# Second attention: value rows broadcast from a copy in DRAM, and the residual x added by TensorE

## The reference

```python
qkv = x @ W_qkv.T                       # 16 heads of 8 features
q = (elu(q) + 1) * scale;  k = elu(k) + 1
for each chunk of 32 tokens:            # causal, state S (8 x 8 a head), Z (8)
    attn = (q @ k.T) * causal
    num = attn @ v + q @ S
    den = attn.sum(-1) + q @ Z
    S = S + k.T @ v;  Z = Z + k.sum(0)
out = num / maximum(den, 1e-6)
x = x + out @ W_out.T
```

## Time and profile before

| | |
|---|---|
| median of 3 runs | 689.75 us (688.23 to 690.7) |
| profiled execution | 690.44 us, its span 688.7 us |
| busy: PE / DVE / ACT / POOL | 378.3 / 424.8 / 219.6 / 358.2 us |
| second attention, first to last period's start | 366.70 to 479.89 us |

### The profile page before, as it was taken

How to read it: one execution, slowest core, us unless ns; L and a number is a source line. 1 busy time by engine, 2 the same in 40 slices (tenths; PEclk the granted TensorE clock), 3 DMA queues, 4 the chain that set the end, 5 groups by cost and what they waited for, 6 DMA issues and landing times.

```text
span 688.7 us, 7801 instructions
## 1 busy us (share of the span) xinstructions
PE 378.3 (55%) x2174; PEld 267.1 (39%) x2174; DVE 424.8 (62%) x1214; ACT 219.6 (32%) x531; POOL 358.2 (52%) x390
## 2 busy tenths in 40 slices
PE   4896755074331678676035667776743217866740
PEld 4554322071111567566012344443321116756640
DVE  6788999997888022123265789999787871222120
ACT  2577000036741122213015334433157312222110
POOL 6037960004100768888214888888740006888753
PEclk9999978577555689988556677877875557999885
DMA  5880000005061223334909988888460712333322
GB/s 148 321 306 0 0 1 0 0 12 172 2 138 2 54 38 45 43 41 36 251 3 121 128 133 131 133 133 131 71 184 0 138 2 53 37 46 45 43 22 19
DMA packets 63721, 54.80 MB, mean 80 GB/s; under 512 B 14656, under 2 KB 52160, under 8 KB 62400
## 3 DMA queue, kind: packets, MB, share of 16 engines
q1 hardware_dynamic: 45824, 44.20, 30.9%
q0 software_dynamic: 11264, 8.99, 10.0%
q10 hardware_dynamic: 6592, 1.15, 1.0%
HBM read 22.27 MB, written 15.27 MB: 55 GB/s over the span
## 4 chain that ended last, share of the span: by engine, by line
DVE 27%; POOL 18%; DMA 17%; issue 15%; PE 13%; ACT 3%; another core or an unknown queue 3%; SPq 2%; DVEq 1%; ACTq 0%; POOLq 0%
DVE arena L1234 11%; DMA arena<-arena 10%; POOL out L531 6%; POOL acc L531 6%; POOL arena L518 3%; DVE arena L1239 3%; DVE tk L1239 3%; DMA out<-arena,idx 2%; PE ps L941 2%; DVE bst L1246 2%; DMA acc<-arena,idx 2%; POOL tb L594 2%; PE ps L1044 1%; DMA tab<-tb 1%
## 5 line engine op out<-in xcount | busy, mean ns | idle before, releaser
L1234 DVE TENSOR_TENSOR arena<-ps,arena 128x256 f32<-128x256 f32 (+1 forms) x82 | 34.1, 425 | 148.0 <-DMA out<-arena,idx 68.3
L518 POOL DMA_INDIRECT arena<-tab,idx x64 | 62.8, 982 | 79.5 <-DMA tab<-tb 30.6
L757 ACT ACTIVATE arena<-ps,b 128x256 f32<-128x256 f32 x128 | 50.1, 474 | 149.5 <-PE ps L1106 135.7
L1106 PE MATMUL ps<-arena,f1w 128*128 128x256 f32 x256 | 74.0, 441 | 14.4 <-DVE arena L1238 12.5
L594 POOL TENSOR_TENSOR tb<-arena 128x512 f32<-128x512 f32 x64 | 70.8, 1122 | 10.1 <-PE ps L1167 9.2
L1116 PE MATMUL ps<-f2w,arena 128*128 128x128 f32 x512 | 65.7, 282 | 6.2 <-issue 4.3
L1116 PEld LDWEIGHTS ps<-f2w,arena 128*128 128x128 f32 x512 | 65.2, 199 | 9.5 <-issue 7.3
L531 POOL DMA_INDIRECT out<-arena,idx x32 | 51.0, 1594 | 24.3 <-DMA out<-arena,idx 12.4
L1106 PEld LDWEIGHTS ps<-arena,f1w 128*128 128x128 f32 x256 | 54.1, 222 | 24.3 <-DVE arena L1238 14.1
L1234 DVE TENSOR_TENSOR arena<-arena 128x256 f32<-128x256 f32 (+22 forms) x109 | 56.8, 555 | 2.2
L531 POOL DMA_INDIRECT acc<-arena,idx x32 | 50.5, 1579 | 13.5 <-issue 8.2
(11 more groups left out here) (265 smaller groups left out, 924.1 us busy)
## 6 DMA issues: line engine op xcount, KB each, us to landing
arena<-arena SPq DMA_DIRECT2D x64, 256.0 KB, 7.2
tab<-tb SPq DMA_DIRECT2D x8, 576.0 KB, 9.0
f1w<-in_f1T SPq DMA_DIRECT2D x4, 1024.0 KB, 12.2
f2w<-in_f2T SPq DMA_DIRECT2D x4, 1024.0 KB, 14.2
acc<-tb SPq DMA_DIRECT2D x8, 256.0 KB, 19.0
arena<-in_f2b SPq DMA_DIRECT2D x2, 1024.0 KB, 5.8
acc<-xs SPq DMA_DIRECT2D x8, 256.0 KB, 6.1
xs<-acc SPq DMA_DIRECT2D x8, 256.0 KB, 6.4
```

Source lines behind the costliest of these rows:

```text
L518: pool.indirect_dma_start(out=XE[:, e % RX, h, :], out_offset=None, in_=tab[f], in_offset=bass.IndirectOffsetOnAxis(ap=idx[:, i:i + 1], ax ...
L757: last = nc.scalar.activation(hT[:, e % 2, t, :], ps[:, 2 * (e % 2) + t // 2, (t % 2) * CAP:(t % 2 + 1) * CAP], ACT.Gelu, bias=b1[:, e, t: ...
L1106: last = nc.tensor.matmul(ps[:, 2 * (e % 2) + t // 2, (t % 2) * CAP:(t % 2 + 1) * CAP], f1w[:, e, t * P:(t + 1) * P], xeT[:, e % 2, :], st ...
L1234: return nc.vector.tensor_tensor(o, a, b, op)
```

## The change

Two edits, independent of each other. First, the values of a group are stored to a DRAM tensor `vd` by one DMA (128 x 512, 256 KB), SP waits until it has landed, and then the eight broadcast DMAs read their rows from `vd`. Only product 0 of group 0 still reads `vT`, and is issued ahead of the first store. Second, `add_out` of DVE is gone. `project_out` on PE now first multiplies the identity with x (128 x 512) into the PSUM bank, and the output projection accumulates on it. ACT copies the sum back to `xs` (`keep_x`), and DVE only takes the statistics (`take_stats`).

```diff
+    vd = nc.dram_tensor("vd", [NG, P, GW], F32).ap()
...
+            def replicate(n, values, i):
+                e = 2 * (i % 4) + i // 4
+                rows = values[e * NH:(e + 1) * NH, :]
+                sp.dma_start(VR[:, i, :], rows.rearrange("h (a t) -> h a t", a=1).to_broadcast([NH, HD, GW])).then_inc(vr_in[i], 16)
             for n in range(NG):
                 sp.wait_ge(v_kept, n + 1)
-                for i in range(HD):
+                if n == 0:
+                    replicate(0, vT[:, 0, :], 0)
+                sp.dma_start(vd[n], vT[:, n % 2, :]).then_inc(v_stored, 16)
+                sp.wait_ge(v_stored, 16 * (n + 1))
+                for i in range(1 if n == 0 else 0, HD):
                     if n >= 1:
                         sp.wait_ge(state_ready, (n - 1) * HD + i + 1)
-                    e = 2 * (i % 4) + i // 4
-                    rows = vT[e * NH:(e + 1) * NH, n % 2, :]
-                    sp.dma_start(VR[:, i, :], rows.rearrange("h (a t) -> h a t", a=1).to_broadcast([NH, HD, GW])).then_inc(vr_in[i], 16)
+                    replicate(n, vd[n], i)
...
+            def keep_x(n):
+                act.wait_ge(fin_prod, n + 1)
+                nc.scalar.activation(xs[:, n * TPG:(n + 1) * TPG, :].rearrange("p t d -> p (t d)"), ps[:, 7, :], ACT.Copy
+                                     ).then_inc(x3_ready, 1)
...
                     keep_normed(n + 1)
+                if n >= 2:
+                    keep_x(n - 2)
                 if n >= 1:
                     spread(n - 1)
...
             def project_out(n):
+                pe.wait_ge(rs_ready, n + 1)
+                nc.tensor.matmul(ps[:, 7, :], ident[:, :], xs[:, n * TPG:(n + 1) * TPG, :].rearrange("p t d -> p (t d)"),
+                                 start=True, stop=False, skip_group_check=True)
                 pe.wait_ge(on_ready, n + 1)
                 for t in range(TPG):
                     last = nc.tensor.matmul(ps[:, 7, t * P:(t + 1) * P], On[:, n % 2, t * P:(t + 1) * P], wou[:, :],
-                                            start=True, stop=True)
+                                            start=False, stop=True, skip_group_check=True)
...
-            def add_out(n):
-                dve.wait_ge(fin_prod, n + 1)
-                row = xs[:, n * TPG:(n + 1) * TPG, :].rearrange("p t d -> p (t d)")
-                tt(row, row, ps[:, 7, :], ALU.add).then_inc(x3_ready, 1)
+            def take_stats(n):
                 dve.wait_ge(x3_ready, n + 1)
                 stats(n)
```

More of the change, by code:

```diff
@@ L216, in build @@
         v_prod, v_kept, state_ready, z_ready = (sem(n) for n in ("v_prod", "v_kept", "state_ready", "z_ready"))
+        v_stored = sem("v_stored")
         vr_in = [sem(f"vr_in{i}") for i in range(HD)]
@@ L845, in _ @@
             keep_raw(1, NG - 2)
+            keep_x(NG - 1)
             keep_raw(1, NG - 1)
@@ L1680, in _ @@
                     if i == 2 and n >= 2:
-                        add_out(n - 2)
+                        take_stats(n - 2)
                     if i == 3 and n + 1 < NG:
```

## The result

| | before | changed |
|---|---|---|
| median (4 runs each) | 690.18 us (688.23 to 690.7) | 678.0 us (677.22 to 678.84) |
| profiled execution, its span | 690.44 us, 688.7 us | 677.22 us, 675.5 us |
| ratio of the times | | 0.983, 95% interval 0.981 to 0.985 |
| period of n = 2 to 6 | 15.96 us | 14.73 us |
| stage: first `take_z` to the issue of the next block's b2 | 134.5 us | 123.3 us |

The changed kernel is 12.2 us faster; 9.2 was forecast. In the two profiled executions the span differs by 13.2 us: 11.2 lie in the second attention, and 2.3 ahead of it, since the first `take_z` stands at 364.36 instead of 366.70 us; behind it 0.3 are lost. The stage's length, not the span, is therefore compared from here on.

A forecast was written before the change was run, and what follows sets the result against it. Prediction: broadcast DMAs set the second attention's pace. Savings 2.9 + 1.2 + 4.8 + 1.0 - 0.7 = 9.2 us, from 689.75 to 680.5 us; own range 677 to 684, 8-in-10 range 673.5 to 687.5.

The forecast's parts named there:

- The broadcasts at 1.0 us: Second attention's broadcast DMAs: a 256 KB tile read from DRAM takes 1.0 us instead of 2.0, as b2's load suggests.
- The rival "DRAM is no faster": Broadcasts: still 2.0 us a tile plus 1.0 for the store, 17.0 us a period, 697 us; chance 0.05.
- Store and reload, 6.5 us hidden: Ahead of each group's first product: two DMA landings, 4.6 to 9.6 us, taken as 6.5, hide behind the group's other work.
- The rival of a new wait at each group's first product: Store and reload replace the DMA wait at the first product; at 9.6 us the kernel takes 692.5 us; chance 0.07.
- n = 0, 2.9 forecast: First group: 3.8 us of DMA waits go, a 0.9 us wait for the second tile comes; 2.9 us saved.
- the reload 3.2 us behind that: First group: the first reload from DRAM lands 3.2 us behind the store's landing, at 369.2 us.
- The identity matmul, 1.1 on the chain: PE's project_out: the added matmul delays the chain by 0.95 or 1.71 us, taken as 1.1.
- the first rival: PE's clock stays at full, its chain does not grow, DVE alone sets 14.3 us a period; 674.5 us; chance 0.20.
- the second: PE's chain stays at half clock, the matmul costs 1.71 us, 15.5 us a period; about 684 us; chance 0.15.
- The period of 15.0: n = 2 to 6: DVE alone 14.3, PE-POOL-DVE loop 14.9, with a sum_own wait taken as 15.0; 4.8 us saved.
- n = 1, 1.2 forecast: Second group: 3.0 us of DMA waits go, POOL's wait for PE takes back up to 2.3; 1.2 us saved.
- n = 7 and the tail, 1.0 - 0.7 = 0.3 forecast: Last group saves 1.0 us like a middle one; behind it the identity matmul holds up project_out, 0.7 us lost.

The follow-up runs named there:

- Experiment 1: Kernel before with only the DRAM copy: add_out stays on DVE, no identity matmul or keep_x; 678.6 against 689.16 us, ratio 0.984.
- experiment 2: Kernel before with only the addition of x moved to PE, broadcasts still read vT; 689.12 against 689.16 us, ratio 1.001.
- experiment 5: Changed kernel without store, broadcasts read 16 rows of vT eight partitions apart (values of other heads and features); 677.21 against 690.71 us, ratio 0.982.
- experiment 6: Changed kernel with each group's store to DRAM made twice, one behind the other; 681.17 against 690.71 us, ratio 0.987.
- experiment 3: Changed kernel with the identity matmul moved ahead of to_xT, into PE's idle time; 675.44 against 689.16 us, ratio 0.980.
- experiment 7: Changed kernel without the identity matmul, x left out of the third block's sum; 675.87 against 690.71 us, ratio 0.980.
- Experiment 4: Changed kernel with product 0 of group 0 read from DRAM too; 676.66 against 689.16 us, ratio 0.982.
- experiment 10: Changed kernel, identity matmul ahead of to_xT and repeated twice in groups 1 to 7, all broadcasts from DRAM; 666.41 against 683.03 us, ratio 0.975.
- experiment 12: Kernel before with spread SBUF rows, no DRAM, early identity matmul, two repeats in groups 1 to 7 and behind the last; 672.33 against 689.23 us, ratio 0.974.
- experiment 11: Changed kernel with products 1, 3, 5 and 7 of every group read from neighbouring vT rows; 676.62 against 683.03 us, ratio 0.989.

## Why the prediction was right

The direction, the mechanism and the order of the bounds were as forecast, and no rival came true as a whole: the time lies 2.5 us under the forecast and inside its own range of 677 to 684. By the prediction's steps:

- **The broadcasts at 1.0 us.** As forecast, from the b2 window: SP's instruction takes 0.6, a transfer about 1.0. Experiment 1 shows the worth of this edit alone, and experiments 2 and 5, one line apart, the reason: neighbouring partitions, not SBUF. The rival "DRAM is no faster" is out.
- **Store and reload, 6.5 us hidden.** Hidden from n = 1 on, and with room: experiment 6 adds 2 us, and DVE waits 0.7 us more in all. The sum came close, its parts did not: the store lands in 2.0 us instead of 3.1, and the reload, read in n = 0, in 3.4 to 4.4 instead of some 3.1, together 5.4 to 6.4. The rival of a new wait at each group's first product is out.
- **n = 0, 2.9 forecast, 1.6 measured.** The step that was off is "the reload 3.2 us behind that". The store landed 5.7 us behind the issue of the first broadcast (363.40 - 357.68), where the prediction had about 5.8; the reload took 4.4 us and not 3.2. DVE's wait became 1.8 us instead of 0.9. Much of this miss is chance: in experiments 1, 3 and 7 the same DMAs gave a reload of 3.4 to 3.9 us, a wait of 0.8 to 1.3 and 2.1 to 2.6 us saved. The prediction also took the first broadcast from `vT` for given. Experiment 4 shows that it was what made the store late: without it n = 0 is shorter by 0.9 to 1.9 us again.
- **The identity matmul, 1.1 on the chain.** It measured 0.7 in the mean, by the chains 6.8 to 7.5 us. The matmul itself takes 1.71 in four of the five groups and 1.46 in one; what varies is how much of the work behind it runs at full clock. The forecast knew both cases (0.95 and 1.71) and took a value between; the trace has two kinds of period instead. Three, at 14.2 to 14.4, are what the first rival was worked out for, two, at 15.3 to 15.5, what the second was (15.5). That their mean lies near the forecast's single value is partly luck.
- **The period of 15.0.** 14.73 in the mean: 1.2 us a period saved instead of 0.96, 6.1 instead of 4.8 in all. DVE alone needs 14.2 (forecast 14.3) and with `add_out` 14.93 (forecast 14.98). The term that was mis-sized is the 0.7 above 14.3: it measured 0.5 above 14.2. In it, DVE's wait for `sum_own` was put at 0.3 us a period and took 0.5 in all five. POOL's waits for `numerator` were to stay as long as before or grow; they shrank a little, from 6.3 to 5.6 us.
- **n = 1, 1.2 forecast, 1.9 measured**, and POOL still waits for `numerator` there; the forecast took the low end of 0.7 to 3.0.
- **n = 7 and the tail, 1.0 - 0.7 = 0.3 forecast, 1.5 measured.** The loss in the tail is there, but smaller: from the start of `transpose_raw` to that of `project_out` it is 1.35 us (484.59 to 485.94), before 0.88 (498.37 to 499.25), so 0.5 is lost and not 0.7. The rest of the stretch thus gained 2.0. Experiment 1, with the DRAM copy alone, gains 0.7 in this stretch, and the rest came with the other edit. Which part of it did that was not taken apart.
- **The rival that the clock stays up.** Not in the changed kernel, where the first 3.5 us of the five chains have 0.50 to 0.60; the one that begins at full, n = 3, falls to half within 1 us. Experiment 3 makes it true in three of five groups by moving work, experiments 10 and 12 in all by adding some, and with it comes the period that was worked out for it: 14.2 against 14.3. The Trainium skill (TensorE: Matmul & The Clock Gate, "Part 1: The HAM clock gate") has it that activity releases the throttle; the rows of experiments 3 and 12 agree, beside that of 7, where less work gave a longer chain.
- **The other half of the change.** The addition on PE was costed as a gain of 0.7 on DVE against 1.1 on PE. Alone it is worth nothing (experiment 2), because DVE then waits for the broadcasts; beside the DRAM copy it is worth 0.6 us of the stage, and 3.7 with its matmul outside the chain (experiment 1 against 3: 123.9 to 120.2); from n = 1 on, 1.6 and 4.2.

The terms sum to 1.6 + 1.9 + 6.1 + 1.5 = 11.1 for the stage (11.2 from its ends), against 9.2. n = 0 came out 1.3 short and the other three 3.2 over, so the misses cancel in part. The medians differ by 12.2; the last microsecond lies within what the profiled executions and the medians vary.

## What to carry to other kernels

When a small transfer out of SBUF is slower than its bytes warrant, look at which partitions it reads: 16 spread over the tile were served as fast as DRAM, 16 neighbours at half that rate or less. Work that an engine can do before a wait should be issued ahead of the wait; on PE it pays twice, as in experiment 3, where the chain behind it then ran at full clock in three of five groups. And a DMA put ahead of another to hide its latency can be what makes it late: in group 0 the first tile made the store take 5.0 us instead of 2.0.

## What the runs showed of the hardware beyond this

- A broadcast of 256 KB took SP 2.0 us of issue from 16 neighbouring partitions of SBUF, 0.72 from 16 spread ones, 0.60 from DRAM (medians).
- A store of 256 KB to DRAM landed in 2.0 us with nothing ahead in its queue, and in 5.0 and 4.2 us behind one slow broadcast (group 0 of the changed kernel, group 1 of experiment 11).
- PE with more to do was sooner done: chains of 7.0 us without the identity matmul, 6.0 with one ahead of them, 5.3 with three, by the granted clock over their first 3.5 us (0.50 to 0.66, 0.53 to 1.00, 1.00).
- The first reload from DRAM landed 3.4 to 4.4 us behind its issue, in five traces with the same burst behind it.
- The start of this stage varied between 360 and 368 us over executions and chips, with nothing changed ahead of it.
